# Eight PSUM banks shared otherwise: three for the ring of attention's scores, two for the ring of front and tail

## What is computed

```python
x = x + 0.5 * _L0_ffn_ref(_layernorm(x, axis=-1), ...)
x = x + _L0_attn_ref(_layernorm(x, axis=-1), L0_attn_W_qkv, L0_attn_W_o)
x = x + 0.5 * _L0_ffn_ref(_layernorm(x, axis=-1), ...)
x = x + 0.5 * _L1_ffn_ref(_layernorm(x, axis=-1), ...)
x = x + _L1_attn_ref(_layernorm(x, axis=-1), L1_attn_Wq, L1_attn_Wk, L1_attn_Wv, L1_attn_Wo)
x = x + 0.5 * _L1_ffn_ref(_layernorm(x, axis=-1), ...)
```

## Time and profile before

| | us |
|---|---|
| median of 3 runs | 3108.23 |
| lowest and highest | 3107.77, 3111.34 |
| profiled execution | 3121.12 |
| span in its trace | 3119.4 |
| PE, DVE, ACT busy in it | 2755.0, 1894.0, 1213.2 |

### The profile page before, as it was taken

How to read it: one execution, slowest core, us unless ns; L and a number is a source line. 1 busy time by engine, 2 the same in 40 slices (tenths; PEclk the granted TensorE clock), 3 DMA queues, 4 the chain that set the end, 5 groups by cost and what they waited for, 6 DMA issues and landing times.

```text
span 3119.4 us, 45976 instructions
## 1 busy us (share of the span) xinstructions
PE 2755.0 (88%) x15374; PEld 1747.3 (56%) x15374; DVE 1894.0 (61%) x5539; ACT 1213.2 (39%) x2706; POOL 743.2 (24%) x1274
## 2 busy tenths in 40 slices
PE   2885899989998998989989998989998999989987
PEld 2563566456655566466655566555664666554544
DVE  6443666665567566665666665675667666666642
ACT  0321243444344343434434443344434344344451
POOL 1321132223222231222322232222322133121110
PEclk8986899999999999999999999999999999999996
DMA  2014103411333113412044113331134212343211
GB/s 56 1 41 124 28 16 67 119 39 31 59 86 93 45 31 63 124 45 57 20 102 119 34 31 66 86 93 43 33 70 124 53 42 34 83 113 88 54 29 42
DMA packets 137424, 193.99 MB, mean 62 GB/s; under 512 B 49439, under 2 KB 111214, under 8 KB 127854
## 3 DMA queue, kind: packets, MB, share of 16 engines
q1 hardware_dynamic: 137198, 191.07, 25.0%
HBM read 122.34 MB, written 67.63 MB: 61 GB/s over the span
## 4 chain that ended last, share of the span: by engine, by line
PE 63%; DVE 13%; DMA 9%; issue 3%; ACT 2%; POOL 2%; SPq 1%; DVEq 0%; ACTq 0%; POOLq 0%
PE bank L728 9%; PE bank L761 7%; PE bank L742 7%; DMA stk<-k_halves 7%; PE bank L564 4%; PE bank L657 4%; PE bank L504 3%; PE bank L544 3%; PE bank L671 3%; PE bank L513 3%; PE bank L495 2%; DVE bank L1080 2%; PE bank L658 2%; PE bank L599 2%; PE bank L681 2%
## 5 line engine op out<-in xcount | busy, mean ns | idle before, releaser
L1283 ACT ACTIVATE pexp<-bank 128x512 f32<-128x512 f32 (+3 forms) x1536 | 675.0, 495 | 604.4 <-PE bank L742 602.6
L728 PE MATMUL bank<-stk,stq 128*128 128x512 f32 (+3 forms) x1536 | 629.9, 424 | 146.2 <-DMA stk<-k_halves 50.0
L1080 DVE CUSTOM_DVE_ANT_0 bank<-bank,maskneg 128x128 f32<-128x128 f32 (+3 forms) x1024 | 501.1, 497 | 418.1 <-PE bank L728 412.0
L728 PEld LDWEIGHTS bank<-stk,stq 128*128 128x128 f32 x1536 | 305.3, 201 | 527.8 <-issue 453.1
L742 PE MATMUL bank<-stq,stk 128*128 128x512 f32 (+3 forms) x1536 | 533.8, 420 | 56.2 <-ACT pexp L1283 52.6
L1083 DVE TENSOR_REDUCE mxa<-bank 128x1 f32<-128x512 f32 x512 | 351.8, 687 | 156.8 <-PE bank L728 151.3
L1431 POOL TENSOR_SCALAR_AFFINE_SELECT pexp<-pexp 128x256 f32<-128x256 f32 x512 | 213.4, 423 | 777.5 <-ACT pexp L1283 777.3
L742 PEld LDWEIGHTS bank<-stq,stk 128*128 128x128 f32 x1536 | 278.9, 200 | 197.2 <-ACT pexp L1283 122.3
L761 PE MATMUL bank<-pexp,vsm 128*32 128x512 f32 (+3 forms) x3072 | 357.0, 539 | 8.8 <-POOL pexp L1431 8.6
L1349 POOL TENSOR_SCALAR_AFFINE_SELECT arena<-arena 128x512 f32<-128x512 f32 x128 | 79.1, 642 | 415.8 <-ACT arena L1187 415.8
L564 PE MATMUL bank<-arena 32*128 32x256 f32 x1024 | 157.1, 426 | 15.3 <-DVE arena L888 11.2
(11 more groups left out here) (183 smaller groups left out, 4192.5 us busy)
## 6 DMA issues: line engine op xcount, KB each, us to landing
stq<-q_halves SPq DMA_DIRECT2D x128, 256.0 KB
arena<-rope_table SPq DMA_DIRECT2D x8, 2048.0 KB
q_halves<-arena SPq DMA_DIRECT2D x32, 512.0 KB, 3.0
k_halves<-arena SPq DMA_DIRECT2D x32, 512.0 KB, 2.8
stk<-k_halves SPq DMA_DIRECT2D x64, 256.0 KB
stk<-k_halves SPq DMA_DIRECT2D x128, 128.0 KB
v_rows<-arena SPq DMA_DIRECT2D x16, 544.0 KB, 4.2
vsm<-v_rows SPq DMA_DIRECT2D x16, 544.0 KB, 3.8
```

The lines of the kernel that those rows point to most:

```text
L728: mm(bk[:, 0:k1 - k0], stq[b_][:, h % 2, qb * P:(qb + 1) * P], stk[b_][:, h % 2, k0:k1], start=True, stop=True).then_inc(s["r_full"], 1)
L1080: nc.vector.tensor_tensor_reduce(out=sc, in0=sc, in1=maskneg[:, CH - (k1 - k0):CH], scale=1.0, scalar=LOWEST, op0=ALU.add, op1=ALU.max, ac ...
L1283: nc.scalar.activation(pexp[:, u % NPX, j, 0:n], ps(j)[:, 0:n], ACT.Exp, scale=DK ** -0.5).then_inc(s["exp_done"], 1)
```

## The change

The ring r gets three banks, `ps(3)` to `ps(5)`, and the ring f two, `ps(6)` and `ps(7)`. In `r_take` the wait is one fill laxer, in `f_take` one fill stricter; the readers look for their data in the new banks. The number of fills, their order, and all instructions and their shapes stay as they were on every engine; in PE's stream other counts of the semaphores are waited for, and `f_free2` is gone.

```diff
-        f_free = [s[f"f_free{i}"] for i in range(3)]
+        f_free = [s[f"f_free{i}"] for i in range(2)]
...
                 def f_take(*key):
                     n = len(ftab)
                     ftab[key] = n
-                    if n >= 3:
-                        nc.tensor.wait_ge(f_free[n % 3], n // 3)
-                    return ps(5 + n % 3)
+                    if n >= 2:
+                        nc.tensor.wait_ge(f_free[n % 2], n // 2)
+                    return ps(6 + n % 2)
 
                 def f_bank(*key):
-                    return ps(5 + ftab[key] % 3)
+                    return ps(6 + ftab[key] % 2)
...
                 def f_freed(*key):
-                    return f_free[ftab[key] % 3]
+                    return f_free[ftab[key] % 2]
 
                 def f_gone(eng, *key):
-                    eng.wait_ge(f_free[ftab[key] % 3], ftab[key] // 3 + 1)
+                    eng.wait_ge(f_free[ftab[key] % 2], ftab[key] // 2 + 1)
 
                 def r_take(*key):
                     n = len(rtab)
                     rtab[key] = n
-                    if n >= 2:
-                        nc.tensor.wait_ge(s["r_used"], n - 1)
-                    return ps(3 + n % 2)
+                    if n >= 3:
+                        nc.tensor.wait_ge(s["r_used"], n - 2)
+                    return ps(3 + n % 3)
 
                 def r_bank(*key):
-                    return ps(3 + rtab[key] % 2)
+                    return ps(3 + rtab[key] % 3)
```

More of the change, by code:

```diff
@@ L340, in macaron @@
                        "y_out").split()
-        plain_names = ("carry st lz f_full f_free0 f_free1 f_free2 stack0 stack1 stack2 stack3 stack4 mrow0 mrow1 v_in r_full r_used "
+        plain_names = ("carry st lz f_full f_free0 f_free1 stack0 stack1 stack2 stack3 stack4 mrow0 mrow1 v_in r_full r_used "
                        "mx_comb m_hl t_ps exp_done causal pv_done ypv_done y_rec rope_in").split()
```

## The result

| | before | after |
|---|---|---|
| median of 4 runs, us | 3109.78 | 3263.44 |
| lowest and highest | 3107.77, 3115.66 | 3261.11, 3269.66 |
| profiled execution, us | 3121.12 | 3262.62 |
| span, us | 3119.4 | 3260.9 |
| PE busy, us | 2755.0 | 2789.9 |

The ratio is 1.049 (95% interval 1.046 to 1.052), so 154 us more. The forecast was 3173 us, with a range up to 3235: the direction was right, the forecast loss was less than half of the measured one, and the time lies outside the range.

A forecast was written before the change was run, and what follows sets the result against it. PE's order of work was taken to bound the kernel. New holes of 126 us after hiding, less 71 gain, plus 10 for the clock, gave +65 on the 3108 us median: 3173 us, range 3090 to 3235.

The forecast's parts named there:

- What bounds the kernel: PE's order of work ends last; its core ring of two banks costs 95.0 us of waits, the other ring little.
- The gain: Core's third bank removes waits before scores and output transposes: 71 us, floor 20, ceiling 95.0.
- The holes: New PE waits in the front and tail ring: 156 us, between 114 and 170; 30 hidden, leaving 126.
- (a): Linear attention, state's product (L575) waits for ACT's copy of the score banks: 56 x 0.73 = 41 us.
- (d): Some 125 other front and tail fills come too early, about half a us each: 62 us, floor 20, ceiling 75.
- (b): Linear attention, blocks 1 to 3: first score-bank pair (L564) waits for ACT's copy of the outputs: 48 x 0.55 = 26 us.
- (c): Linear attention: second score-bank pair waits for another stream's fill or its own first pair: 53 x 0.5 = 27 us.
- The clock: More holes in PE's work lower its granted clock: 10 us, with 0 and 40 as ends.
- The one on the clock: Rival: holes pull PE's clock down or readers queue, 40 to 77 us instead of 10: 3203 to 3240 us, chance 0.20.
- The faster one: Rival: late front and tail fills fall into existing PE waits while freed score waits are kept: 3077 us, chance 0.16.
- the even trade: Rival: other late fills at their floor, 30 us hidden, gain of 84: 3108 us; chance 0.09 with the no-change rival.
- Nothing changes: Rival: the bank isn't what PE waits for, DVE's pace binds throughout; shares chance 0.09 with the even trade.

The follow-up runs named there:

- the strict kernel: Kernel before, three banks for front and tail, each of their fills also waiting until the fill two before was read out; core's ring keeps two: 3334.72 us, ratio 1.071.
- The three parts alone: Kernel before with the stricter wait for only the state's product (3163.45 us), only the linear attention's score-bank pairs (3216.98), or only all other front and tail fills (3165.87).
- filler in the holes: Changed kernel with the core's ring back at two banks, plus 168 unread matmuls ahead of the linear attention's fills that can come too early: 3256.77 us.
- the strict waits of the rest alone: Kernel before with the stricter wait only for front and tail fills other than the state's product and the score-bank pairs: 3165.87 us, ratio 1.016.
- the shared ring: Kernel before with all fills, core's and front's, taking turns on one ring of five banks in PE's order: 2997.67 us, ratio 0.963.
- four shared banks: The one ring for all fills with four banks in place of five, one PSUM bank unused: 3028.31 us, ratio 0.974.
- The same matmuls elsewhere: Two banks for each ring, with the 168 unread matmuls ahead of feed-forward fills instead of the linear attention's: 3356.88 us.
- shared ring, state later: The one ring of five banks for all fills, with the state's product one step later in PE's order: 3002.41 us, ratio 0.965.
- The strict waits of the state's product and of the pairs: Two runs, kernel before with the stricter wait only for the state's product (3163.45 us, ratio 1.016) or only for the score-bank pairs (3216.98 us, ratio 1.034).

## Why the prediction was wrong, by its own steps

- **What bounds the kernel** was right: PE's order, with the core's ring costing 95 us and the other ring next to nothing.
- **The gain**, 71 us of 95: 71 us in time, from the difference between the strict kernel and the changed one. The number was right by luck, since its make-up wasn't. The prediction thought of idle time. By the traces PE's idle time fell by 16 us only (487 to 471), since it then waited longer for exponentials (49.9 to 62.3) and other things, and busy time by 52 (2842.4 to 2789.9). Some 30 of the 52 are the clock's ((584 - 525) / 2) and 23 are matmuls that took less time at the same level (the scores' busy time fell from 641.7 to 601.2 us). That what is freed is partly lost to the next wait was said; that PE's matmuls would get shorter by it wasn't.
- **The holes**, terms (a) to (d): (a) 41 forecast, 41.3 measured; (b) 26 and 28.0; (b) and (c) together 53, where the idle time before L564 grew by 61 (15.3 to 76.4); (d) 62, where idle time grew by 45 with those waits alone. In the kernel with strict waits alone, the net of idle time is +123 us against 126 forecast, after 30 for what is hidden. The three parts alone make 146 us, so 23 of them are hidden behind each other; whether the prediction's 30 is right for the reason that it gave, waits for exponentials and for Pool, no run tells. The wait for exponentials went from 52.6 to 49.9 us only, and in the changed kernel, which has the third bank too, other waits didn't shrink but grew: its idle time rose by 107 us, where the prediction had a net of 55.
- **The clock** is the step that failed: 10 us, with 40 as the end. The loss alone made PE busy for 87 us longer, 82 of them by the clock, and 126 - 71 + 87 = 142 is the difference of the spans, 141.5. In the changed kernel itself, where the gain of 71 is spread as said above, the same 141.5 us are 107 of idle time and 52 of clock, less 18 by matmuls that took less time at the same level. The working had three faults. It took the one fall looked at, after 1.9 us of idling, for the pattern and held holes of 0.5 to 0.7 us to be harmless, though the 1.9 us were themselves a sum of several holes, the longest of 1.42 us; it scaled by the net of holes (55 us), though the freed waits and the new holes lie in different places; and it took a small part of even that. Scaled by the loss's own 126 us, the same working gives 151 x 126 / 209 = 91 us; the 151 us are what 0.94 in the earlier trace rows leaves of the middle's 2520 us. The 10 us themselves were an estimate that no run shows: in their place stand the 52 us of the changed kernel and the 82 of the loss alone. The prediction's own signs of being wrong on the clock, 0.92 or less in the middle and PE busy for over 30 us more, both came (0.92 and 35). The middle's clock was 0.94 before, 0.91 with the strict waits, and 0.94 with filler in the holes, though the strict waits of the rest alone added 45 us of idle time and left the pulses not granted at 251 us. With the upper end of the prediction's clock term, 40 us, its sum is 3203 us: nearer, and still too low by 60.
- **The rivals.** The one on the clock is what happened, and beyond its upper end of 3240. The faster one and the even trade fall: (c) and (d) weren't hidden. "Nothing changes" falls with the 71 us that the third bank gave. The comparison of fills with reads that sized the holes was sound in the sum; the range failed because the term on the clock was bounded by scaling a mean and not by what one more hole does.
- The remaining 12 us between 142 and the 154 of the medians are the profiled execution of before, which was 11 to 13 us above its median.

## What to carry to other kernels

Short holes on a TensorE that is otherwise full were paid twice here: once as idle time, and up to 0.7 times again (82 us for 123) as slower matmuls at the lower clock (0.894 over the span, where it was 0.917). It isn't so for every hole: one kind, 45 us of idle time in all, left the clock as it was. So read the granted clock beside the idle time, over several executions, and don't net freed waits against new ones before the clock is thought of. A change of busy time isn't all clock either (40 of 85 us in the shared ring): split it by the granted level first. For two rings of PSUM banks, one shared ring in TensorE's order, with a count for each bank, is worth a try: here four shared banks (3028 us) beat both splits of five (3112 and 3263).

## What the chip showed that was not expected

- 168 matmuls that nobody reads, 72 us of work or more on the bounding engine, made the kernel 78 us faster (3334.7 to 3256.8 us), by filling holes of 0.5 to 0.7 us; the granted clock went from 0.894 to 0.919. The same matmuls elsewhere made it 22 us slower, and even there the clock rose, to 0.904.
- Busy time of the same 15374 matmuls ran from 2663 us (shared ring, state later, clock 0.933) over 2755 (before, 0.917) to 2842 (strict waits, 0.894): a spread of 179 us that no count of instructions shows. 135 of them are the clock's (314 and 584 us busy at the lower level); the other 44 are there at the same level.
- Holes differ in what they cost beside themselves. The strict waits of the state's product and of the pairs, 41 and 60 us of idle time, raised the pulses not granted by 24 and 51 us, as means of four executions; those of the rest, 45 us of idle time, left them at 251. Together with the others the rest did cost clock (357 us, against 321 without it). What sets the kinds apart was not tried.
